# Vision tower: attention 1 value products in groups of four heads, 32 columns each, with the row sums in a bank of their own

## The chip, the cores and the metric

The kernel runs on one core of a Trainium2 chip. The time is the device time of one execution in microseconds (us). Before the change three runs took 4316.67, 4334.95 and 4337.84 us; the median is 4334.95 us.

## The reference

64 images pass through one block: patch embedding with two layer norms and a class token (197 tokens of 192 numbers), a first attention with 12 heads of 64 dims, and a second part that is a router with eight rank-16 adapters on the qkv projection and again an attention with 12 heads, of 16 dims each. Both halves are added to a residual. The change is in the first attention; its core is

```python
qkv = x @ w_qkv.T                       # (b, 197, 3 * 12 * 64)
q = q * rsqrt(norm over heads(q) + EPS) # k likewise
dots = einsum('bhid,bhjd->bhij', q, k)
scores = softmax(dots / scale[:, None, None], axis=-1)
out = einsum('bhij,bhjd->bhid', scores, v)
out = out.transpose(0, 2, 1, 3).reshape(b, n, h * dh) @ w_out.T + b_out
```

Here `h` is the head, `i` the query token, `j` the key token and `d` the dim.

## The kernel before

Everything is written by hand: one instruction stream per engine, with semaphores. The table `ORDER` lists the steps of half a pass; each engine walks through the same table and does its own part of every step. Half a pass is done for buffer set s = 0 and once more for s = 1, and a loop repeats the pair. A step with a minus sign belongs to the other set's image, so that two images are under way, half a pass apart: while the first attention of one runs, the second attention of the image before it, and the embedding of the one after it, run between its steps. `@n` is the PSUM bank of a step's product (there are eight); steps in `WIDE` take two banks.

The steps of the first attention that matter here, for pair i of heads 2i and 2i+1 (i = 0 to 5):

- `ST.i`: the scores with the keys as rows, 99 keys at a time (two key tiles t), on TensorE (lines 545 to 563); ScalarE then takes the exponential from PSUM into one of four buffers `ebuf` (line 732). The buffers go round over both attentions' exponentials.
- `PV.i` (line 574): TensorE multiplies the values with `ebuf`. The result has the dims in PSUM rows and the queries in columns: head e of the pair in rows 64e to 64e+63. One group of four matmuls (2 key tiles x 2 heads) gives the values; four more with a block of ones in place of the values (`ones_col`, 64 wide) give, in the same bank, the row sums, repeated in 64 rows. They are float32 and 197 columns wide. Each float32 matmul has two records of the profile, so a step of 8 matmuls shows as 16. Then ScalarE makes 1/sum as exp(-ln(sum)) (lines 740 and 741) into `rinv`.
- `M.i` (line 943): VectorE multiplies the two into `o_t`, which lies in the first half of `qk`.
- `OP` (line 586): the output projection, on six tiles of 128 rows of `o_t`.

The second attention's `PV2.i` (line 633) takes four heads at once, each in 32 columns (16 dims, 16 ones), and takes the sums out of the same product. `OP2` is its projection, `T1` the transposes of the next image, `LA`, `LB`, `LC` its layer norm steps on VectorE and GpSimd.

An engine does its steps strictly in the order of the table: a step of ScalarE that waits holds all the steps behind it.

Of the kernel before, what the change touches and what calls it, by code (L numbers as in the profile page):

```python
# [27 lines left out]
NT = NP + 1  # L28
PD, KC = 768, 6
TR, TO = 99, 98  # L30
# [18 lines left out]
-X -OP@2 QK.0@4 -LD -T2@3 QK.1@0 -G@7 QK.2@4 -GB S -EMB@7 -T3@2 PS@6 N.0 -QK2.0@6 N.1 -QK2.1@0  # L49
N.2 -V2@2 -SM2.0@4 -SM2.1@2 N.3 -SM2.2@0 V.0@4 -SM2.3@2 -SM2.4@0 -SM2.5@6 V.1@4 SM.0@0 -NT2@7  # L50
SM.1@2 SM.2@4 -ST2.0@0 SM.3@6 -ST2.1@2 SM.4@0 SM.5@4 -ST2.2@6 -PV2.0@3 -M2.0 NT@0 -ST2.3@6
-ST2.4@2 -ST2.5@4 -PV2.1@6 ST.0@0 -PV2.2@4 ST.1@2 -LA ST.2@6 PV.0@4 M.0 PV.1@5 ST.3@0 -M2.1
ST.4@2 PV.2@6 -LB M.1 -M2.2 ST.5@0 PV.3@2 M.2 M.3 PV.4@3 PV.5@6 M.4 -LC M.5 -OP2@1 -T1@3
"""


# [13 lines left out]
EMBEDDING = ("X", "EMB", "LA", "LB", "LC", "T1")  # L70
BEHIND = {p for p in SCHED[:len(SCHED) // 2] if p[1] == 1 and p[0] not in EMBEDDING}
AHEAD = {p for p in SCHED if p[1] == 0 and p[0] in EMBEDDING}
WIDE = ("QK", "V", "SM", "ST", "QK2", "SM2", "ST2")
EBUFS = 4


# [58 lines left out]
def vit_tower(nc, x_t, w_emb, ln1, ln1_bias, tok_const, tok_bias, w_qk, w_v, w_out, w_gl, w_qkv2, w_lora_b,  # L135
# [4 lines left out]
    with ctx:  # L140
        def sb(name, shape, dt=F32):
            return ctx.enter_context(nc.sbuf_tensor(name, shape, dt))
# [55 lines left out]
        ss = two("ss", [128, 2, NT])  # L198
        nrm = [ss[s][:].rearrange("p a t -> p (a t)") for s in range(2)]
        hn2_t = [ss[s][0:HC] for s in range(2)]  # L200
        vx_both = sb("vx", [TR, 2, 2, H, DH])
        vx = [vx_both[:, s] for s in range(2)]
        ones_col = sb("ones_col", [TR, DH])
        mx = two("mx", [TR, 2, H])
        neg = two("neg", [TR, 2, 128])
        ebuf = [sb(f"ebuf{i}", [TR, 2, 2, NT]) for i in range(EBUFS)]
# [78 lines left out]
        neg_copied = signal("neg_copied", ("NT2",))  # L285
        mx2_ready = signal("mx2_ready", ("NT2",))
        res_ready = rd_sig["OP2"]
        rr_ready = signal("rr_ready", ("PS",))
        rinv_ready = signal("rinv_ready", ("PV",))
        sums2_ready = rd_sig["PV2"]  # L290
# [29 lines left out]
        def passes(eng, body):  # L320
            body(Pass("start", -1))
            body(Pass("first", 0))
            with eng.Fori(1, ITERS - 1) as it:
# [2 lines left out]
            body(Pass("last", ITERS))  # L326

        loads = [(emb_raw, w_emb), (ln1_sb, ln1), (ln1b_raw, ln1_bias), (tokc, tok_const), (tok_b, tok_bias), (qk_raw, w_qk),
                 (v_raw, w_v), (out_w, w_out), (gl_w, w_gl), (qkv2_raw, w_qkv2), (lorab_raw, w_lora_b),
                 (bias2_raw, w_bias2), (proj_w, w_proj), (scale_sb, scale), (rowc, row_const),  # L330
                 (mats_sb, mats), (sel_raw[0:64], head_rows[64:128]), (sel_raw[64:128], head_rows[64:128])]
        e_order = [p for p in SCHED if p[0] in ("ST", "ST2")]
        pv_order, pv2_order = steps["made_PV"], steps["made_PV2"]

# [6 lines left out]
            return (xss_ready, p) if p[0] == "X" else (ss_ready, ("S", p[1], 0))  # L341

        def exp_used(p):
            q = ("PV", p[1], p[2]) if p[0] == "ST" else ("PV2", p[1], p[2] // 2)
            return pe_sig[q[0]], q

        def tile_cols(t):
# [101 lines left out]
        def _(pe):  # L449
# [34 lines left out]
            def body(now):  # L484
                for p in now.steps():
# [87 lines left out]
                                mm = nc.tensor.matmul(o, kb[s][:, h, tile_cols(t)], qb[s][:, g, 0:NT],  # L573
                                                      start=False, stop=True)
                    elif kind == "PV":
                        wait(pe, now, rd_sig["ST"], ("ST", s, i))
                        wait(pe, now, rd_sig["V"], ("V", s, 1))
                        eb = ebuf[e_order.index(("ST", s, i)) % EBUFS]
                        for at in (0, NT):
                            for t in range(2):  # L580
                                n = key_rows(t)
                                for e in range(2):
                                    left = vx[s][0:n, t, 2 * i + e, :] if at == 0 else ones_col[0:n]
                                    mm = nc.tensor.matmul(ps(p, slice(DH * e, DH * e + DH), slice(at, at + NT)),  # L584
                                                          left, eb[0:n, e, t, :], start=(t == 0), stop=(t == 1))
                    elif kind == "OP":
                        wait(pe, now, rd_sig["PV"], ("M", s, 5))
                        for t in range(2):
                            for m in range(H // 2):
                                mm = nc.tensor.matmul(ps(p, slice(0, TR), slice(D * t, D * t + D)),  # L590
# [65 lines left out]
        def _(act):  # L656
# [13 lines left out]
            def body(now):  # L670
                act.sem_clear(act_chain)
                count[0] = 0
                for p in now.steps():
# [36 lines left out]
                    elif kind == "N" and i % 2 == 1:  # L710

                        wait(act, now, qkn_ready, ("N", s, i - 1))
                        high = (qh, kh)[i // 2]
                        nc.scalar.copy(high[:, :, 0:NT], qk[s][:, 6 * (i // 2):6 * (i // 2) + 6, :]
                                       ).then_inc(high_N[1], 1)
                    elif kind == "V":
                        wait(act, now, pe_sig[kind], p)
                        nc.scalar.mul(  # L718
                            vx[s][:, i].rearrange("p (b h) d -> p b h d", b=2),
                            psum[0:TR, b:b + 2, 0:INNER // 2].rearrange("p b (h d) -> p b h d", d=DH),  # L720
                            1 / WS).then_inc(done, 1)
                    elif kind == "NT":
                        wait(act, now, pe_sig[kind], p)
                        nc.scalar.copy(neg_t[s][:, 0:NT], psum[:, b, 0:NT]).then_inc(done, 1)
                    elif kind == "NT2":
                        wait(act, now, pe_sig[kind], p)
                        nc.scalar.copy(qb[s][64:128, 0, 0:NT], psum[64:128, b, 0:NT]).then_inc(neg_copied[1], 1)
                    elif kind in ("ST", "ST2"):
                        wait(act, now, pe_sig[kind], p)
                        n = e_order.index(p)  # L730
                        wait_free(act, now, e_users[n % EBUFS], exp_used)
                        nc.scalar.activation(ebuf[n % EBUFS][:].rearrange("p e a t -> p e (a t)"),  # L732
                                             psum[0:TR, b:b + 2, 0:2 * NT], ACT.Exp).then_inc(done, 1)
                    elif kind == "PV":

                        wait(act, now, pe_sig[kind], p)
                        n = pv_order.index(p) % 2
                        wait_free(act, now, rinv_users[n], reader)
                        r = rinv[n][:]
                        link(nc.scalar.activation(r, psum[:, b, NT:2 * NT], ACT.Ln))  # L740
                        nc.scalar.activation(r, r, ACT.Exp, scale=-1.0).then_inc(rinv_ready[1], 1)  # L741
                    elif kind == "PV2":
                        wait(act, now, sums2_ready, p)
                        r = sums2[pv2_order.index(p) % 2][:]
                        link(nc.scalar.activation(r, r, ACT.Ln))
                        nc.scalar.activation(r, r, ACT.Exp, scale=-1.0).then_inc(rinv2_ready[1], 1)
                    elif kind == "G":

                        wait(act, now, gmax_ready, p)
                        nc.scalar.activation(gates[s][:, :, 0:NE], gl[s][:, :, 0:NE], ACT.Exp  # L750
                                             ).then_inc(gexp_ready[1], 1)
                    elif kind == "T3":
                        wait(act, now, pe_sig[kind], p)
                        nc.scalar.copy(comb_t[s][:, 0:NT], psum[0:3 * (NE + 1), b, NT:2 * NT])
                        nc.scalar.copy(hw_s[s][:, 0, 0:NT], psum[:, b, 0:NT]).then_inc(split_T3[1], 1)
                    elif kind == "QK2":
                        wait(act, now, pe_sig[kind], p)

                        dst, f = (qa[s], QSCALE / WS) if i == 0 else (high2, 1 / WS)
                        if i == 1:  # L760
                            wait_free(act, now, high2_users, reader)
                        nc.scalar.mul(dst[:, 0:2, 0:NT],
                                      psum[:, b, 0:2 * NT].rearrange("p (m t) -> p m t", m=2), f)
                        nc.scalar.mul(dst[:, 2, 0:NT], psum[:, b + 1, 0:NT], f).then_inc(high_QK2[1], 1)
                        if i == 1:

                            wait(act, now, high_QK2, p)
                            for j in range(4):
                                a = nc.scalar.mul(ka[s][:].rearrange("p (g j) t -> p g j t", j=4)[:, :, j, :],  # L769
                                                  high2[:], masks[:, j:j + 1])  # L770
# [10 lines left out]
        def _(dve):  # L781
# [59 lines left out]
            def body(now):  # L841
                dve.sem_clear(dve_chain)
                count[0] = 0
                for p in now.steps():
# [92 lines left out]
                    elif kind == "M":  # L937
                        done, q = rd_sig["PV"][1], ("PV", s, i)
                        b = BANK[q]

                        wait(dve, now, rinv_ready, q)
                        r = rinv[pv_order.index(q) % 2]
                        nc.vector.tensor_tensor(o_t[s][:, i, :], psum[:, b, 0:NT], r[:], ALU.mult  # L943
                                                ).then_inc(done, 1)
                    elif kind == "OP":

# [162 lines left out]
```

## Time and profile before

| | before |
|---|---|
| median of three runs | 4334.95 us |
| the profiled execution's own time | 4333.73 us |
| its span (first to last instruction) | 4331.8 us |
| TensorE matmuls busy | 3840.3 us, 89% |
| VectorE busy | 2706.7 us, 62% |
| ScalarE busy | 2232.1 us, 52% |
| GpSimd busy | 524.0 us, 12% |
| mean granted TensorE clock | 0.953 |

The profile is of one execution. Busy time is the union of an engine's instructions. Matmuls overlap each other in the record, and the time of one record is not its cost: the distance from the start of a group of them to the start of the next is.

### The profile page before, as it was taken

The page shows a single profiled execution, that of the slowest core. Times are in us where ns is not written, and L with a number is a line of the kernel's source. Part 1 is how long each engine was busy: PE and PEld are TensorE (multiplying, and loading weights), DVE is VectorE, ACT ScalarE, POOL GpSimd, SP SyncE. Part 2 cuts the span into 40 slices and gives each one's busy share as a digit, 9 for nine tenths or more (in the row PEclk, how much of TensorE's full clock was granted, in tenths as well). Part 3 has the DMA queues.
Part 4 walks back from the last instruction along what each step waited for, and adds up shares of the span by engine and source line. Part 5 has one row for each costly group of instructions (what it writes and reads, how often), then busy time and mean ns, then how long its engine had stood idle before and what let it go on. Part 6 is the DMA issues. An engine that isn't in the chain of part 4 may idle for free.

```text
span 4331.8 us, 98533 instructions
## 1 busy us (share of the span) xinstructions
PE 3840.3 (89%) x38552; PEld 3175.7 (73%) x38552; DVE 2706.7 (62%) x6866; ACT 2232.1 (52%) x3969; POOL 524.0 (12%) x858
## 2 busy tenths in 40 slices
PE   4999998889988998989999889899888898899888
PEld 3777777777777777777777777777777777777776
DVE  4666666566566666665665666666656656656654
ACT  1555555555555555545545555555555555555553
POOL 1110111111101101101111011011111111111110
PEclk7999999999999999999999999999999999999997
DMA  2000000000000000000000000000000000000000
GB/s 76 8 16 8 16 8 15 15 10 14 15 8 15 16 8 15 15 8 15 8 15 16 8 15 15 8 16 15 9 15 10 14 15 10 14 15 8 15 4 4
DMA packets 26198, 60.41 MB, mean 14 GB/s; under 512 B 3534, under 2 KB 16465, under 8 KB 25714
## 3 DMA queue, kind: packets, MB, share of 16 engines
q1 hardware_dynamic: 25806, 54.14, 4.1%
q8 instruction: 377, 6.18, 0.6%
q14 instruction: 15, 0.09, 0.0%
HBM read 44.45 MB, written 9.68 MB: 12 GB/s over the span
## 4 chain that ended last, share of the span: by engine, by line
PE 72%; DVE 17%; issue 4%; ACT 4%; POOL 1%; DMA 0%; SPq 0%; DVEq 0%; ACTq 0%; POOLq 0%
PE psum L584 13%; DVE mx L922 9%; PE psum L590 7%; PE psum L513 6%; PE psum L523 6%; PE psum L618 6%; PE psum L496 6%; PE psum L557 5%; PE psum L541 3%; PE psum L648 3%; PE psum L641 2%; PE psum L620 2%; PE psum L621 2%; ACT ka L769 2%; PE psum L571 2%
## 5 line engine op out<-in xcount | busy, mean ns | idle before, releaser
L922 DVE TENSOR_REDUCE mx<-psum 99x4 f32<-99x788 f32 x768 | 707.2, 972 | 67.3 <-PE psum L541 40.3
L732 ACT ACTIVATE ebuf<-psum 99x788 f32<-99x788 f32 x768 | 605.8, 825 | 175.7 <-PE psum L573 163.9
L513 PE MATMUL psum<-hn_s,qk_w 96*128 96x197 f16 x4608 | 435.8, 252 | 1.2 <-DVE hn_s L888 1.2
L440 POOL TENSOR_TENSOR veps<-mv,eps_ln 99x2 f32<-99x2 f32 x256 | 49.9, 195 | 3169.2 <-DVE mv L831 2552.9
L696 ACT ACTIVATE qk_sq<-psum 128x788 f32<-128x788 f32 x192 | 159.1, 828 | 516.0 <-PE psum L513 516.0
L513 PEld LDWEIGHTS psum<-hn_s,qk_w 96*128 96x128 f16 x4608 | 406.2, 99 | 8.8 <-DVE hn_s L888 1.5
L618 PE MATMUL psum<-hn_s,qkv_w 96*128 96x197 f16 x2304 | 342.2, 254 | 44.2 <-ACT ss L705 43.1
L523 PE MATMUL psum<-v_w,hn_s 96*99 96x384 f16 x1536 | 333.6, 376 | 30.3 <-DVE mx L922 21.8
L943 DVE TENSOR_TENSOR qk<-psum,rinv 128x197 f32<-128x197 f32 x384 | 137.9, 359 | 342.1 <-ACT rinv L741 342.1
L590 PE MATMUL psum<-out_w,qk 128*99 128x192 f32 x1536 | 286.8, 348 | 61.5 <-issue 61.3
L584 PE MATMUL psum<-ebuf,vx 98*64 98x197 f32 (+1 forms) x3072 | 332.6, 336 | 0.0
L571 PE MATMUL psum<-qa,ka 128*99 128x197 f16 x1536 | 288.9, 252 | 46.8 <-DVE qb L934 31.3
L584 PE MATMUL psum<-ebuf,ones_col 98*64 98x197 f32 (+1 forms) x3072 | 323.3, 330 | 0.0
L590 PEld LDWEIGHTS psum<-out_w,qk 128*99 128x99 f32 x1536 | 264.9, 178 | 72.1 <-issue 66.4
L541 PE MATMUL psum<-ka,qa 128*99 128x197 f16 x1536 | 209.7, 298 | 110.5 <-ACT ka L769 100.7
L523 PEld LDWEIGHTS psum<-v_w,hn_s 96*99 96x99 f16 x1536 | 216.3, 147 | 113.8 <-DVE mx L922 29.9
L620 PE MATMUL psum<-hw_s,lorab_w 128*128 128x197 f16 x1152 | 290.7, 252 | 0.0
L718 ACT ACTIVATE vx<-psum 99x768 f32<-99x768 f32 x128 | 103.9, 812 | 352.6 <-PE psum L523 352.6
L573 PE MATMUL psum<-qb,kb 128*99 128x197 f16 x1536 | 282.7, 248 | 0.0
L541 PEld LDWEIGHTS psum<-ka,qa 128*99 128x99 f16 x1536 | 182.0, 156 | 133.7 <-issue 55.4
L496 PE MATMUL psum<-emb_w,xb 128*99 128x193 f32 x1536 | 263.9, 327 | 12.6 <-DVE emb_b L821 12.6
L618 PEld LDWEIGHTS psum<-hn_s,qkv_w 96*128 96x128 f16 x2304 | 189.2, 99 | 116.8 <-ACT ss L705 83.3
(164 smaller groups left out, 8006.3 us busy)
## 6 DMA issues: line engine op xcount, KB each, us to landing
xb<-x_t SPq DMA_DIRECT2D x64, 591.0 KB, 3.8
out<-h SPq DMA_DIRECT2D x128, 73.5 KB
vx<-w_qk SPq DMA_DIRECT2D x1, 1152.0 KB
out<-h SPq DMA_DIRECT2D x64, 0.8 KB
qk<-w_qkv SPq DMA_DIRECT2D x1, 720.0 KB
qk_sq<-w_emb SPq DMA_DIRECT2D x1, 576.0 KB
v_raw<-w_v SPq DMA_DIRECT2D x1, 576.0 KB
out_w<-w_out SPq DMA_DIRECT2D x1, 576.0 KB
```

Of the source, the lines that this page charges most:

```text
L496: nc.tensor.matmul(ps(p, slice(0, TR), slice(194 * t, 194 * t + D + 1)), xb[s][:, c, tile_cols(t)], emb_w[:, c, :], start=(c == 0), stop=( ...
L513: mm = nc.tensor.matmul(ps(p, slice(0, 128), slice(at, at + NT), m // 2), qk_w[:, w, c, f:f + 128], hn_s[s][:, v, c, 0:NT], start=(n == 0) ...
L523: mm = nc.tensor.matmul(ps(p, slice(0, TR), slice(0, INNER // 2), b), hn_s[s][:, v, c, tile_cols(i)], v_w[:, w, c, INNER // 2 * b:INNER // ...
L541: mm = nc.tensor.matmul(ps(p, slice(0, TR), slice(NT * t, NT * t + NT), e), qa[s][:, h // 4, tile_cols(t)], ka[s][:, h, 0:NT], start=True, ...
L571: nc.tensor.matmul(o, ka[s][:, h, tile_cols(t)], qa[s][:, g, 0:NT], start=True, stop=False)
L573: mm = nc.tensor.matmul(o, kb[s][:, h, tile_cols(t)], qb[s][:, g, 0:NT], start=False, stop=True)
L584: mm = nc.tensor.matmul(ps(p, slice(DH * e, DH * e + DH), slice(at, at + NT)), left, eb[0:n, e, t, :], start=(t == 0), stop=(t == 1))
L590: mm = nc.tensor.matmul(ps(p, slice(0, TR), slice(D * t, D * t + D)), o_t[s][:, m, tile_cols(t)], out_w[:, m, :], start=(m == 0), stop=(m ...
L618: nc.tensor.matmul(o, qkv2_w[:, w, c, f], hn2_s[s][:, v, c, 0:NT], start=(c + w + v == 0), stop=False)
L620: nc.tensor.matmul(o, lorab_w[:, w, f], hw_s[s][:, v, 0:NT], start=False, stop=False)
L732: nc.scalar.activation(ebuf[n % EBUFS][:].rearrange("p e a t -> p e (a t)"), psum[0:TR, b:b + 2, 0:2 * NT], ACT.Exp).then_inc(done, 1)
L922: nc.vector.tensor_reduce(mx[s][:, :, 2 * i:2 * i + 2].rearrange("p a e -> p e a"), psum[0:TR, b:b + 2, 0:2 * NT].rearrange("p e (a t) -> ...
```

## The change

The six `PV` steps of an image become three, each over four heads. A head's 64 dims are taken in two halves of 32 (c = 0, 1). Head j of the four has the 32 PSUM rows 32j to 32j+31, for both halves and for the sums; the halves stand side by side in the first bank, the sums (c = 2) alone in the second. The sums are made first and have a semaphore of their own (`sums_made`), on which ScalarE waits. VectorE's multiply takes both halves at once, with one `rinv` for both, and waits for the values too. The dims of `o_t` stand in another order now, so the rows of `out_w` are loaded in that order, by eight DMAs in place of one, at the end of the list of loads. A step now needs the exponentials of two `ST` steps. In the table the three new steps stand behind `ST.2`, `ST.4` and `ST.5`.

```diff
--ST2.4@2 -ST2.5@4 -PV2.1@6 ST.0@0 -PV2.2@4 ST.1@2 -LA ST.2@6 PV.0@4 M.0 PV.1@5 ST.3@0 -M2.1
-ST.4@2 PV.2@6 -LB M.1 -M2.2 ST.5@0 PV.3@2 M.2 M.3 PV.4@3 PV.5@6 M.4 -LC M.5 -OP2@1 -T1@3
+-ST2.4@2 -ST2.5@4 -PV2.1@6 ST.0@0 -PV2.2@4 ST.1@2 -LA ST.2@6 PV.0@4 M.0 ST.3@0 -M2.1
+ST.4@2 PV.1@6 -LB M.1 -M2.2 ST.5@4 PV.2@2 -LC M.2 -OP2@1 -T1@7
-WIDE = ("QK", "V", "SM", "ST", "QK2", "SM2", "ST2")
+WIDE = ("QK", "V", "SM", "ST", "PV", "QK2", "SM2", "ST2")
-        ones_col = sb("ones_col", [TR, DH])
+        ones_col = sb("ones_col", [TR, DH // 2])
+        sums_made = signal("sums_made", ("PV",))
         loads = [...
-                 (v_raw, w_v), (out_w, w_out), (gl_w, w_gl), ...
+                 (v_raw, w_v), (gl_w, w_gl), ...
+        for j in range(4):
+            for c in range(2):
+                loads.append((out_w[32 * j:32 * j + 32, c::2, :],
+                              w_out[64 * (j % 2) + 32 * c:64 * (j % 2) + 32 * c + 32, j // 2::2, :]))
                     elif kind == "PV":
-                        wait(pe, now, rd_sig["ST"], ("ST", s, i))
+                        wait(pe, now, rd_sig["ST"], ("ST", s, 2 * i + 1))
                         wait(pe, now, rd_sig["V"], ("V", s, 1))
-                        eb = ebuf[e_order.index(("ST", s, i)) % EBUFS]
-                        for at in (0, NT):
+                        for c in (2, 0, 1):
                             for t in range(2):
                                 n = key_rows(t)
-                                for e in range(2):
-                                    left = vx[s][0:n, t, 2 * i + e, :] if at == 0 else ones_col[0:n]
-                                    mm = nc.tensor.matmul(ps(p, slice(DH * e, DH * e + DH), slice(at, at + NT)),
-                                                          left, eb[0:n, e, t, :], start=(t == 0), stop=(t == 1))
+                                for j in range(4):
+                                    eb = ebuf[e_order.index(("ST", s, 2 * i + j // 2)) % EBUFS]
+                                    left = (vx[s][0:n, t, 4 * i + j, 32 * c:32 * c + 32] if c < 2
+                                            else ones_col[0:n])
+                                    mm = nc.tensor.matmul(
+                                        ps(p, slice(32 * j, 32 * j + 32), slice(NT * (c % 2), NT * (c % 2) + NT), c // 2),
+                                        left, eb[0:n, j % 2, t, :], start=(t == 0), stop=(t == 1))
+                            if c == 2:
+                                mm.then_inc(sums_made[1], 1)
...
-                        wait(act, now, pe_sig[kind], p)
+                        wait(act, now, sums_made, p)
...
-                            link(nc.scalar.activation(r, psum[:, b, NT:2 * NT], ACT.Ln))
+                            link(nc.scalar.activation(r, psum[:, b + 1, 0:NT], ACT.Ln))
...
                         wait(dve, now, rinv_ready, q)
+                        wait(dve, now, pe_sig["PV"], q)
-                        nc.vector.tensor_tensor(o_t[s][:, i, :], psum[:, b, 0:NT], r[:], ALU.mult
+                        nc.vector.tensor_tensor(o_t[s][:, 2 * i:2 * i + 2, :],
+                                                psum[:, b, 0:2 * NT].rearrange("p (c t) -> p c t", c=2),
+                                                r[:].unsqueeze(1).broadcast_to([128, 2, NT]), ALU.mult
```

Two places show what moves. The first is TensorE's stream in the loop's half pass for s = 1, around the end of `ST.2` and `PV.0`. `ebuf2`, `ebuf3`, `ebuf0`, `ebuf1` hold the exponentials of `ST.0`, `ST.1`, `ST.2`, `ST.3` there; `vx` are the values. Before:

```order
L561 MATMUL psum<-neg_t1,head_sel 99x197 x2
L584 MATMUL psum<-ebuf2,vx 64x197 x4
L584 MATMUL psum<-ebuf2,ones_col 64x197 x4
L584 MATMUL psum<-ebuf3,vx 64x197 x4
L584 MATMUL psum<-ebuf3,ones_col 64x197 x4
L557 MATMUL psum<-qh,kh 99x197 x2
```

and of the change (line 584 is line 591 now, 557 is 563, 561 is 567):

```order
L567 MATMUL psum<-neg_t1,head_sel 99x197 x2
L591 MATMUL psum<-ebuf2,ones_col 32x197 x2
L591 MATMUL psum<-ebuf3,ones_col 32x197 x2
L591 MATMUL psum<-ebuf2,ones_col 32x197 x2
L591 MATMUL psum<-ebuf3,ones_col 32x197 x2
L591 MATMUL psum<-ebuf2,vx 32x197 x2
L591 MATMUL psum<-ebuf3,vx 32x197 x2
L591 MATMUL psum<-ebuf2,vx 32x197 x2
```

The step started with `ebuf2` alone and came to `ebuf3` after eight matmuls; now `ebuf3` is needed by the third matmul, and the step waits for it ahead of its first.

The second place is ScalarE's stream from the exponential of `ST.1` on (`ebuf3`), in the loop's half pass for s = 0. Before:

```order
L732 ACTIVATE ebuf3<-psum 99x788
L308 REGISTER_ALU
L732 ACTIVATE ebuf0<-psum 99x788
L740 ACTIVATE rinv0<-psum 128x197
L741 ACTIVATE rinv0<-rinv0 128x197
L740 ACTIVATE rinv1<-psum 128x197
L741 ACTIVATE rinv1<-rinv1 128x197
L308 REGISTER_ALU
L732 ACTIVATE ebuf1<-psum 99x788
L308 REGISTER_ALU
L732 ACTIVATE ebuf2<-psum 99x788
```

and of the change (732 is 742, 740 and 741 are 750 and 751, the register instruction of 308 is that of 310):

```order
L742 ACTIVATE ebuf3<-psum 99x788
L310 REGISTER_ALU
L742 ACTIVATE ebuf0<-psum 99x788
L750 ACTIVATE rinv0<-psum 128x197
L751 ACTIVATE rinv0<-rinv0 128x197
L310 REGISTER_ALU
L742 ACTIVATE ebuf1<-psum 99x788
L310 REGISTER_ALU
L742 ACTIVATE ebuf2<-psum 99x788
L750 ACTIVATE rinv1<-psum 128x197
L751 ACTIVATE rinv1<-rinv1 128x197
```

The order of the exponentials is as it was; the second pair of `rinv` instructions ahead of `ebuf1` is gone. Over a half pass three pairs are left of six.

## Rows read from the trace of the kernel before

**Rows 1.** The page: busy time, and the chain that ended last by engine and line.

```profile
PE 3840.3 (89%) x38552; PEld 3175.7 (73%) x38552; DVE 2706.7 (62%) x6866; ACT 2232.1 (52%) x3969; POOL 524.0 (12%) x858
...
PE 72%; DVE 17%; issue 4%; ACT 4%; POOL 1%; DMA 0%; SPq 0%; DVEq 0%; ACTq 0%; POOLq 0%
```

**Rows 2.** Chain of waits, one half pass's value products (start us, us, what).

```profile
2081.58 0.86 PE psum L641 x16
2082.44 0.39 PE psum L557 x6
...
2083.25 0.81 PE psum L641 x16
...
2085.55 2.84 PE psum L584 x32
...
2089.89 1.49 PE psum L584 x16
...
2092.19 4.18 PE psum L584 x48
2096.37 2.12 PE psum L648 x12
```

**Rows 3.** TensorE's timeline, same half pass (start us, us, what, idle before).

```profile
2085.49 0.89 PE L584 MATMUL psum<-ebuf,vx 98*64 98x197 f32 x8
2086.21 0.84 PE L584 MATMUL psum<-ebuf,ones_col 98*64 98x197 f32 x8
```

**Rows 4.** ScalarE's timeline, same half pass.

```profile
2085.63 0.81 ACT L732 ACTIVATE ebuf<-psum 99x788 f32<-99x788 f32 x1
...
2089.25 1.55 ACT L732 ACTIVATE ebuf<-psum 99x788 f32<-99x788 f32 x2
2091.42 0.34 ACT L740 ACTIVATE rinv<-psum 128x197 f32<-128x197 f32 x1 [0.63 <-PE psum L584]
...
2092.24 0.83 ACT L732 ACTIVATE ebuf<-psum 99x788 f32<-99x788 f32 x1
```

**Rows 5.** ScalarE's timeline, an exponential for which TensorE waits.

```profile
2080.63 0.83 ACT L732 ACTIVATE ebuf<-psum 99x788 f32<-99x788 f32 x1
```

**Rows 6.** TensorE's weight loads that waited for it.

```profile
2081.53 0.35 PEld L641 LDWEIGHTS psum<-ebuf,v 98*32 98x32 f32 x12 [0.16 <-ACT ebuf L732]
```

**Rows 7.** VectorE's timeline, the half pass of rows 2.

```profile
2088.42 0.66 DVE L837 TENSOR_SCALAR h<-hn,mv,rstd 99x192 f32<-99x192 f32 x2
...
2090.95 0.25 DVE L831 BATCH_NORM_AGGREGATE mv<-st 99x2 f32<-99x6 f32 x2
```

**Rows 8.** Groups (line, engine, op, shapes, count | busy us, mean ns | idle before).

```profile
L943 DVE TENSOR_TENSOR qk<-psum,rinv 128x197 f32<-128x197 f32 x384 | 137.9, 359 | 342.1 <-ACT rinv L741 342.1
...
L888 DVE TENSOR_TENSOR hn_s<-psum,hn_s 96x394 f16<-96x394 f32 x128 | 72.5, 567 | 120.3 <-ACT hn_s L690 120.3
...
L641 PEld LDWEIGHTS psum<-ebuf,v 99*32 99x32 f32 x1536 | 53.0, 111 | 11.5
```

**Rows 9.** Timeline of the program's start: DMA issues, VectorE's first work.

```profile
3.87 0.42 SPq L360 DMA_DIRECT2D out_w<-w_out  x1
...
8.62 3.85 SPq L360 DMA_DIRECT2D qk_sq<-sel  x2
...
27.25 1.36 DVE L792 TENSOR_TENSOR emb_w<-qk_sq,ln_sb 128x1152 f32<-128x1152 f32 x1 [27.25 <-DMA qk_sq<-sel]
```

**Rows 10.** Half passes (us; busy PE, PEld, DVE, ACT, POOL; PEclk; DMA).

```profile
3294.74:3360.50 65.76, 57.62 (x605) 47.57 (x603) 41.87 (x108) 34.90 (x62) 8.41 (x14) 1.00 0.06 19
3360.50:3424.18 63.68, 58.67 (x605) 48.74 (x603) 41.98 (x107) 34.80 (x62) 7.77 (x13) 0.97 0.03 7
1837.33:1906.87 69.54, 62.07 (x605) 50.95 (x603) 41.98 (x107) 34.90 (x62) 8.43 (x14) 0.93 0.06 19
```

**Rows 11.** TensorE's timeline, behind three of its longest waits.

```profile
1862.79 1.52 PE L541 MATMUL psum<-ka,qa 128*99 128x197 f16 x12 [1.59 <-ACT ka L769]
1864.71 4.08 PE L523 MATMUL psum<-v_w,hn_s 96*99 96x384 f16 x12 [0.41 <-DVE mx L922]
...
2042.54 0.52 PE L480 MATMUL psum<-mats_sb,hn 98*96 98x98 f32 x4 [1.46 <-DVE hn L837]
...
2070.48 2.15 PE L523 MATMUL psum<-v_w,hn_s 96*99 96x384 f16 x12
```

**Rows 12.** Granted clock of stretches of TensorE (us; busy; PEclk; DMA).

```profile
1862.00:1863.00 1.00, 0.21 (x3) 1.00 0.00 0
...
1864.00:1869.00 5.00, 4.59 (x17) 0.50 0.00 0
...
2085.49:2096.30 10.81, 10.81 (x146) 1.00 0.01 3
```

**Rows 13.** The line that ends OP on VectorE, once per half pass.

```profile
L950 DVE TENSOR_TENSOR h<-psum,h x64: 557/558/559, 122.2 to 4277.2; 99x384 f32<-99x384 f32 x64
```

More of the change, by code:

```diff
@@ L328, in vit_tower @@
         loads = [(emb_raw, w_emb), (ln1_sb, ln1), (ln1b_raw, ln1_bias), (tokc, tok_const), (tok_b, tok_bias), (qk_raw, w_qk),
-                 (v_raw, w_v), (out_w, w_out), (gl_w, w_gl), (qkv2_raw, w_qkv2), (lorab_raw, w_lora_b),
+                 (v_raw, w_v), (gl_w, w_gl), (qkv2_raw, w_qkv2), (lorab_raw, w_lora_b),
                  (bias2_raw, w_bias2), (proj_w, w_proj), (scale_sb, scale), (rowc, row_const),
                  (mats_sb, mats), (sel_raw[0:64], head_rows[64:128]), (sel_raw[64:128], head_rows[64:128])]
+        for j in range(4):
+            for c in range(2):
+                loads.append((out_w[32 * j:32 * j + 32, c::2, :],
+                              w_out[64 * (j % 2) + 32 * c:64 * (j % 2) + 32 * c + 32, j // 2::2, :]))
         e_order = [p for p in SCHED if p[0] in ("ST", "ST2")]
@@ L343, in exp_used @@
         def exp_used(p):
-            q = ("PV", p[1], p[2]) if p[0] == "ST" else ("PV2", p[1], p[2] // 2)
+            q = ("PV", p[1], p[2] // 2) if p[0] == "ST" else ("PV2", p[1], p[2] // 2)
             return pe_sig[q[0]], q
@@ L575, in body @@
                     elif kind == "PV":
-                        wait(pe, now, rd_sig["ST"], ("ST", s, i))
+                        wait(pe, now, rd_sig["ST"], ("ST", s, 2 * i + 1))
                         wait(pe, now, rd_sig["V"], ("V", s, 1))
-                        eb = ebuf[e_order.index(("ST", s, i)) % EBUFS]
-                        for at in (0, NT):
+                        for c in (2, 0, 1):
                             for t in range(2):
                                 n = key_rows(t)
-                                for e in range(2):
-                                    left = vx[s][0:n, t, 2 * i + e, :] if at == 0 else ones_col[0:n]
-                                    mm = nc.tensor.matmul(ps(p, slice(DH * e, DH * e + DH), slice(at, at + NT)),
-                                                          left, eb[0:n, e, t, :], start=(t == 0), stop=(t == 1))
+                                for j in range(4):
[7 more added lines that the diff above has]
+                                mm.then_inc(sums_made[1], 1)
                     elif kind == "OP":
-                        wait(pe, now, rd_sig["PV"], ("M", s, 5))
+                        wait(pe, now, rd_sig["PV"], ("M", s, 2))
                         for t in range(2):
```

## The prediction, made before the changed kernel ran

> **What bounds the kernel now.** I read the page first: matmuls are busy 89% of the span, and the chain that ended last runs 72% over TensorE, 17% over VectorE and 4% over ScalarE [rows 1]. So a microsecond matters if it lies on TensorE's stream, and in stretches where TensorE does not itself wait. Then I read the chain of waits in the stretch of the value products. It stays on TensorE from end to end: step after step, without a wait, from PV2 to the end of the six PV steps and on to OP2 (L648) [rows 2]. There TensorE alone sets the pace, and ScalarE follows it: it is idle 0.63 us before a 1/sum [rows 4]. Shorter value products would therefore shorten every half pass in full, unless a new wait appears. There are 64 half passes, one per image.
>
> **The value products on TensorE.** The six steps stand in three groups of the chain, of two, one and three steps: 2.84, 1.49 and 4.18 us, together 8.51 us [rows 2]. Each further step adds 1.345 us, ((4.18 - 1.49) / 2), so a group has 0.145 us at its start and 8 matmuls of 64 columns take 1.345 us. The price of 32 columns is in PV2, which already puts four heads side by side: 8 matmuls, 0.81 us [rows 2], less the 0.145 us at the start 0.665 us, half of the wide ones. A new step has 24 such matmuls: 0.145 + 3 x 0.665 = 2.14 us; three steps 6.42 us. Gain 8.51 - 6.42 = 2.09 us per image, 134 us in all. This is what the change would bring if nothing else moved. The unknown is whether the rate of PV2 holds over 24 matmuls in a row; below it can't go (197 columns are streamed at the same pace), above it could come to one weight load after the other, 111 ns each [rows 8], two records per matmul: 48 x 0.111 = 5.33 us per step. I take the rate of PV2, because its 16 loads, at the same 111 ns each, are within its 0.81 us, and 12 of them take 0.35 us together [rows 6].
>
> The row shows that the loads of neighbouring column groups overlap. The Trainium skill says otherwise (TensorE: Matmul & The Clock Gate, Part 3, The mechanism): weight loads overlap running matmuls only if they are for other rows of the array, and all of these take the same rows. By that rule the step would come to the 5.33 us above. The trace disagrees with it in PV2; I keep it as a rival for the longer run.
>
> **The waits that it adds.** TensorE stops for a step until the exponentials of two ST steps are there, not one. What comes behind it in its stream (the next ST, and with it the next exponential) stops too. I move the stretch of [rows 2] through, with these durations: from the end of an exponential to the effective start of the step that waits for it 0.17 us (exponential over at 2080.63 + 0.83 = 2081.46 [rows 5], the step behind it over at 2082.44, and it takes 0.81 [rows 2]: 2082.44 - 0.81 - 2081.46); an exponential 0.83 us, the last one of ST.5 starting 0.86 us after ST.5 itself (2092.24 [rows 4], 2089.89 + 1.49 = 2091.38 [rows 2]); ST.5 0.81 us (2092.19 - 2091.38), ST.3 and ST.4 together 1.50 us (2089.89 - 2088.39).
> - PV.0 could start at 2085.55. It needs the exponential of ST.1, which ScalarE runs from 2085.63 to 2086.44 [rows 4]; it starts at 2086.61. Wait 1.06 us. Before, TensorE was at the first pair's products meanwhile [rows 3]. It ends at 2088.75.
> - ST.3 and ST.4 run to 2090.25. The exponential of ST.3 starts 0.86 us after ST.3, at 2089.61, and ends at 2090.44. PV.1 starts at 2090.61: wait 0.36 us; it ends at 2092.75.
> - ST.5 runs to 2093.56. Its exponential runs from 2093.61 to 2094.44, and PV.2, the very next step, needs it: start 2094.61, wait 1.05 us, end 2096.75. Before, three steps were left here and only the last needed ST.5.
>
> OP2 starts at 2096.75 and not at 2096.37 [rows 2]. The three waits (2.47 us) eat the gain (2.09 us) and 0.38 us more. Times 64 this is +24 us. The waits scale with nothing that the change makes faster: each is one exponential and its hand-over, behind an ST that TensorE has just made.
>
> **The other parts.** ScalarE has three pairs of 1/sum fewer, and starts them when the sums are made. It takes work from an engine that waits for TensorE here; the exponentials that TensorE now waits for don't stand behind the removed pairs (ST.1's is ahead of them, ST.3's starts when its scores are made). Gain nothing; had ScalarE been late it would be 0.34 to 0.7 us. VectorE's six multiplies of 0.359 us become three over 394 columns, at the 0.567 us of such a read from PSUM [rows 8]: 0.45 us less per image, off the path. But M.0 now waits for the values to 2088.8 and holds LB behind it: LB begins about 2089.8 (0.57 and M2.1 later) and not at 2088.42, and takes 2.8 us to its last instruction (2088.42 to 2091.20 [rows 7]), so to 2092.6; M.1 can't begin before that anyway. LC follows at about 2094, and T1, which needs it, comes behind OP2 at 2098.9. The last M.2 ends by 2097.5, OP starts behind OP2 and T1 (2096.75 + 2.12 + about 0.35), some 1.7 us later. These cost nothing; that 1.7 us is the cover. Banks: a step takes two, all of them free in time (ST.5 takes bank 4 when M.0 has long read it). The rows of `ones_col` and the order of `out_w` change no count.
>
> The start: all engines wait for the last constant, at 27.25 us. Seven more DMAs are issued behind what is last now. An issue takes 0.42 us for `out_w`, and 3.85 us for the two of `sel` [rows 9]: +2.9 us, between 0 (bandwidth is the limit) and 13 (7 x 1.9). I take 2.9, the row of the same tensor.
>
> **The sum.** It is made against the profiled execution's 4333.73 us (span 4331.8 and 1.9 around it), which is 1.2 us under the median of the three runs: 4333.7 + 24.3 + 2.9 = 4361 us. A change under 0.5%, 22 us, can't be told from none here; 4361 is 26 us over the median, so just beyond.
>
> **The clock.** The granted clock decides between kinds of half passes. Of equal work, two in a row took 65.76 and 63.68 us at clock 1.00 and 0.97, another of the first kind 69.54 us at 0.93 [rows 10]. The low clock (1.2 GHz for 2.4) sets in soon after TensorE's longest waits: after 1.59 us idle the clock was 0.50 for 5 us, and the twelve matmuls of L523 took 4.08 us for 2.15; after a wait of 1.46 us elsewhere it stayed at full speed [rows 11, 12]. The same wait has it in one half pass and not in the next, so it hangs on how the waits fall in time, and a half pass of another length changes that. The mean half pass is (4277.2 - 122.2) / 63 = 65.95 us [rows 13], a pair 131.9, between the quick pair (65.76 + 63.68 = 129.4) and the slow one (69.54 + 63.68 = 133.2). In the value products themselves the clock was 1.00 with TensorE never idle [rows 12]; the new waits, at most 1.06 us with 2.1 us of work or more between them, are shorter than those in front of a low clock.
>
> The Trainium skill (TensorE: Matmul & The Clock Gate, HAM oscillation) holds only waits longer than any in this loop for harmful. By it there would be no loss to shift; the trace disagrees, the clock falls after 1.59 us.
>
> **The rivals.**
> - The pairs become quick ones more often (faster side). All 32 quick: 32 x (131.9 - 129.4) = 80 us less than the forecast, 4281 us. For it: quick and slow pairs are about equally common now. Against: nothing in the change shortens the waits that bring the low clock. Half-way, 4321. It is faster beyond 0.5% from about two thirds of the way.
> - The pairs become slow ones more often: 32 x (133.2 - 131.9) = 42 us more, 4403 us. For it: three new waits.
> - The waits don't show, because the exponentials come earlier than I have them: 4333.7 - 134 + 2.9 = 4203 us. Against: [rows 4] has the start of ST.1's exponential fixed by ScalarE's order, untouched.
> - The narrow matmuls don't hold their rate over 24, up to loads one after another: 3 x 64 x (5.33 - 2.14) = 612 us more, 4973 us; from 2.26 us per step on it adds over 22 us. Against: PV2's rows.
> - The new waits bring the low clock once per image: 64 x (4.08 - 2.15) = 124 us more, 4485 us. Against: their length.
>
> **How the numbers follow.** The forecast, waits of 2.5 us against a gain of 2.1, has 0.60, with a range of its own of 4328 to 4390 (hand-over of 0.17 us left out three times is -33 us; an exponential 0.1 us later each time +19 and the start at 13 in place of 3 +10). Quick pairs 0.12, slow pairs 0.14, waits hidden 0.05, rate lost 0.04, low clock in the new waits 0.05. The range 4318 to 4405 leaves out the last three, and the far end of quick pairs. Slower than 4356.6 (+0.5%): 0.37 of my own case's 0.60, all but little of the 0.14, and 0.09, together 0.59. Faster than 4313: 0.05 and 0.09 of the quick pairs, 0.14. Same: 0.27.
>
> **What would show it.** Right: in TensorE's timeline a wait for the exponential (L742) of about 1 us before the first and the third value step, some 0.3 us before the second; a step of 48 records that takes 2.1 to 2.2 us; OP2 0.3 to 0.5 us later relative to the end of ST.2; about 150 us more of TensorE's idle time put down to ScalarE's exponential, and matmul busy time down by about 130 us. ScalarE busy down by 192 x 0.71 = 136 us with no effect. Wrong: waits under 0.5 us, value steps over 2.3 us, a granted clock off 0.953 by more than 0.01, or constants landing later than 32 us.

## The result: 2.1% slower, and the profile after

The changed kernel takes 4426.37 us (median of four runs, 4401.76 to 4442.45); the kernel before took 4336.4 us in the runs beside it (4316.67 to 4338.45). The ratio is 1.0213, 95% interval 1.0153 to 1.0273. Forecast were 4361 us, 4318 to 4405: the direction is right, and the loss is 90 us where 26 were expected. The profiled execution has a span of 4440.7 us against 4331.8.

The page of the changed kernel, busy time and the shares of the chain [rows 1]:

```profile
PE 3802.5 (86%) x41624; PEld 3145.2 (71%) x41624; DVE 2683.7 (60%) x6674; ACT 2096.0 (47%) x3585; POOL 523.8 (12%) x858
...
PE 67%; DVE 19%; ACT 7%; issue 5%; POOL 1%; SPq 0%; DMA 0%; DVEq 0%; ACTq 0%; POOLq 0%
```

ScalarE is down by the 136 us expected. TensorE's matmuls are down by only 38 us, though the value products alone went from 655.9 to 466.5 us: other matmuls took longer. One group of them, with not one matmul more, before and after:

```profile
L523 PE MATMUL psum<-v_w,hn_s 96*99 96x384 f16 x1536 | 333.6, 376 | 30.3 <-DVE mx L922 21.8 <-ACT vx L718 8.5
```

```profile
L529 PE MATMUL psum<-v_w,hn_s 96*99 96x384 f16 x1536 | 399.0, 430 | 48.7 <-DVE mx L932 40.1 <-ACT vx L728 8.5
```

The mean granted clock is 0.936, from 0.953.

The value products in the chain of waits, a stretch that answers to [rows 2] (start us, us, what):

```profile
3888.27 0.85 PE psum L651 x16
...
3890.65 0.81 ACT ebuf L742
3891.46 0.24 issue
3891.71 2.22 PE psum L591 x48
...
3894.78 0.84 ACT ebuf L742
3895.62 0.09 issue
3895.71 2.22 PE psum L591 x48
...
3898.79 0.84 ACT ebuf L742
3899.63 0.09 issue
3899.72 2.22 PE psum L591 x48
3901.94 2.12 PE psum L658 x12
```

In front of each value step the chain leaves TensorE for an exponential of ScalarE (L742). TensorE's timeline has the three waits, of 1.13, 0.29 and 0.97 us (in brackets, idle before the row):

```profile
3891.71 0.88 PE L591 MATMUL psum<-ebuf,ones_col 98*32 98x197 f32 x16 [1.13 <-ACT ebuf L742]
...
3895.71 0.88 PE L591 MATMUL psum<-ebuf,ones_col 98*32 98x197 f32 x16 [0.29 <-ACT ebuf L742]
...
3899.72 0.88 PE L591 MATMUL psum<-ebuf,ones_col 98*32 98x197 f32 x16 [0.97 <-ACT ebuf L742]
...
3901.87 2.19 PE L658 MATMUL psum<-proj_w,qk 128*99 128x192 f32 x12
```

Measured from ST.1's exponential, which begins at 3890.64 here and at 2085.63 in [rows 4], OP2 begins 11.23 us later where it began 10.67 us later (3901.87 - 3890.64; [rows 2] with the 0.07 us that the two views differ by): 0.56 us lost per half pass, where 0.38 were forecast. That is 36 us in 64 half passes at the most; the rest of the 90 must be elsewhere. Half passes, from the end of OP to the next, two pairs of one execution, the common kind first (columns as in [rows 10]):

```profile
1136.03:1202.48 66.45, 58.41 (x653) 48.39 (x651) 41.61 (x104) 32.67 (x56) 7.77 (x13) 0.95 0.03 7
1202.48:1272.49 70.01, 60.34 (x653) 49.93 (x651) 41.59 (x104) 32.78 (x56) 8.45 (x14) 0.93 0.05 17
3648.87:3714.32 65.45, 55.69 (x653) 46.24 (x651) 41.50 (x105) 32.77 (x56) 8.43 (x14) 1.00 0.06 20
3714.32:3778.58 64.26, 56.82 (x653) 47.38 (x651) 41.59 (x104) 32.68 (x56) 7.77 (x13) 0.97 0.03 7
1163.01:1169.84 6.83, 6.36 (x26) 4.92 (x27) 5.07 (x6) 1.55 (x2) 0.00 (x0) 0.50 0.00 0
1207.39:1210.80 3.41, 3.41 (x21) 3.25 (x19) 0.52 (x1) 1.44 (x2) 0.00 (x0) 0.50 0.02 5
1186.80:1198.60 11.80, 10.54 (x190) 8.97 (x183) 5.79 (x16) 4.49 (x10) 1.89 (x3) 1.00 0.01 3
```

The quick pair takes 65.45 + 64.26 = 129.71 us, 0.27 us more than the quick pair of before (129.44, [rows 10]). But most pairs, some 20 of 31, are of another kind, 66.45 + 70.01 = 136.46 us, which the trace of the kernel before does not have: its slow pairs mostly took 133.2, its longest 135.1. The last three rows say where: the clock is at half speed (0.50, 1.2 GHz) for 6.8 us from 27 us behind OP on, and for 3.4 us from 5 us behind it, while in the stretch with the value products and their new waits it is 1.00. TensorE's timeline at the first place shows what stands ahead of it:

```profile
1161.54 1.21 PE L547 MATMUL psum<-ka,qa 128*99 128x197 f16 x12 [1.66 <-ACT ka L779]
1163.48 4.08 PE L529 MATMUL psum<-v_w,hn_s 96*99 96x384 f16 x12 [0.73 <-DVE mx L932]
```

It is the wait of SM2.0 for `ka`; the one in [rows 11] is of 1.59 us, with the same 4.08 us behind it. The change does not touch these steps. Nor does the wait bring the low clock each time: in the quick pair of the same execution it stands there too, and the twelve matmuls of L529 take 2.15 us.

```profile
3674.31 1.20 PE L547 MATMUL psum<-ka,qa 128*99 128x197 f16 x12 [1.58 <-ACT ka L779]
3676.24 2.15 PE L529 MATMUL psum<-v_w,hn_s 96*99 96x384 f16 x12 [0.73 <-DVE mx L932]
```

The line that ends OP gives the mean, (4385.8 - 121.2) / 63 = 67.69 us per half pass, 1.74 more than the 65.95 of before [rows 13]; 1.74 x 63 = 110 us are the whole difference of the two spans (109 us).

```profile
L963 DVE TENSOR_TENSOR h<-psum,h x64: 556/558/559, 121.2 to 4385.8; 99x384 f32<-99x384 f32 x64
```

The start of the program has little to do with it: the last constant lands 1.2 us later than in [rows 9].

```profile
28.42 1.36 DVE L802 TENSOR_TENSOR emb_w<-qk_sq,ln_sb 128x1152 f32<-128x1152 f32 x1 [28.42 <-DMA out_w<-w_out]
```

### The profile page after: what moved, and what is told of

It reads as the page before. It is cut to its first block, busy times and chain, and to the rows that moved or that the text cites. A ratio compares the mean times of both kernels' runs of the same rounds, so it can differ in the third digit from the quotient of the medians.

```text
span 4440.7 us, 104158 instructions
## 1 busy us (share of the span) xinstructions
PE 3802.5 (86%) x41624; PEld 3145.2 (71%) x41624; DVE 2683.7 (60%) x6674; ACT 2096.0 (47%) x3585; POOL 523.8 (12%) x858
## 4 chain that ended last, share of the span: by engine, by line
PE 67%; DVE 19%; ACT 7%; issue 5%; POOL 1%; SPq 0%; DMA 0%; DVEq 0%; ACTq 0%; POOLq 0%
PE psum L591 10%; DVE mx L932 9%; PE psum L529 8%; PE psum L519 7%; PE psum L600 6%; PE psum L628 6%; PE psum L502 6%; ACT ebuf L742 4%; PE psum L658 3%; PE psum L547 3%; PE psum L563 3%; PE psum L651 2%; PE psum L630 2%; DVE kb L1030 2%; PE psum L610 2%
## 5 line engine op out<-in xcount | busy, mean ns | idle before, releaser
L742 ACT ACTIVATE ebuf<-psum 99x788 f32<-99x788 f32 x768 | 605.3, 825 | 344.1 <-PE psum L567 182.2
L519 PE MATMUL psum<-hn_s,qk_w 96*128 96x197 f16 x4608 | 454.1, 257 | 1.2 <-DVE hn_s L898 1.2
L529 PE MATMUL psum<-v_w,hn_s 96*99 96x384 f16 x1536 | 399.0, 430 | 48.7 <-DVE mx L932 40.1
L519 PEld LDWEIGHTS psum<-hn_s,qk_w 96*128 96x128 f16 x4608 | 419.3, 101 | 12.5 <-DVE hn_s L898 1.5
L529 PEld LDWEIGHTS psum<-v_w,hn_s 96*99 96x99 f16 x1536 | 250.3, 170 | 160.0 <-DVE mx L932 53.2
L954 DVE TENSOR_TENSOR qk<-psum,rinv 128x394 f32<-128x394 f32 x192 | 109.2, 569 | 367.0 <-PE psum L591 367.0
L600 PE MATMUL psum<-out_w,qk 128*99 128x192 f32 x1536 | 261.6, 327 | 44.5 <-issue 44.2
L591 PE MATMUL psum<-ebuf,vx 98*32 98x197 f32 (+1 forms) x6144 | 298.3, 330 | 0.0
L591 PE MATMUL psum<-ebuf,ones_col 98*32 98x197 f32 (+1 forms) x3072 | 168.2, 334 | 151.8 <-ACT ebuf L742 151.5
L600 PEld LDWEIGHTS psum<-out_w,qk 128*99 128x99 f32 x1536 | 245.0, 166 | 49.8 <-issue 49.2
L547 PEld LDWEIGHTS psum<-ka,qa 128*99 128x99 f16 x1536 | 191.0, 161 | 125.8 <-issue 55.1
```

The costliest lines, as they stand in the source:

```text
L519: mm = nc.tensor.matmul(ps(p, slice(0, 128), slice(at, at + NT), m // 2), qk_w[:, w, c, f:f + 128], hn_s[s][:, v, c, 0:NT], start=(n == 0) ...
L529: mm = nc.tensor.matmul(ps(p, slice(0, TR), slice(0, INNER // 2), b), hn_s[s][:, v, c, tile_cols(i)], v_w[:, w, c, INNER // 2 * b:INNER // ...
L547: mm = nc.tensor.matmul(ps(p, slice(0, TR), slice(NT * t, NT * t + NT), e), qa[s][:, h // 4, tile_cols(t)], ka[s][:, h, 0:NT], start=True, ...
L591: mm = nc.tensor.matmul(ps(p, slice(32 * j, 32 * j + 32), slice(NT * (c % 2), NT * (c % 2) + NT), c // 2), left, eb[0:n, j % 2, t, :], sta ...
```

## The experiments

Two questions were put: how much of the 90 us is the clock, and what moves it. Two tools serve them. A filler is a row of matmuls whose result the step itself overwrites:

```python
def fill(p, n):
    for _ in range(n):
        nc.tensor.matmul(ps(p, slice(0, 128), slice(0, NT)), qk_w[:, 0, 0, 0:128],
                         qk_w[:, 0, 0, 0:NT], start=True, stop=True)
```

Put ahead of a wait, and no longer than it, it fills idle time and adds nothing to the chain; put behind it (a padding) it is added work.

**1. The kernel before, padded by four matmuls.**

```diff
                         wait(pe, now, o2_ready, ("M2", s, 2))
+                        fill(p, 4)
```

> The kernel before, with four more float16 matmuls of 197 columns (they write OP2's own bank, which OP2 then overwrites) in front of the six projections of OP2, once per half pass: about 0.34 us of matmuls and up to 0.15 us for one more change between float16 and float32, so 0.34 to 0.5 us later from OP2 on. That is about the delay that the change has at the same place (0.56 us in its trace). Theory A (the loss is mostly the clock: any small delay per half pass moves the loop into an alignment in which the low clock comes in both half passes): clearly more than the 22 to 32 us of the added work, 40 to 100 us over the kernel before, with a granted clock under 0.950. Theory B (the new waits for the exponentials themselves, or the narrow matmuls, cost the 90 us): 22 to 32 us, clock 0.953 as before.

Measured: 4327.94 us against 4326.64 for the kernel before on the same chip, ratio 1.0005 (0.9984 to 1.0026), clock 0.955. Neither came: not the 22 us of work, and not the loss. That any small delay upsets the clock is false; theory A was narrowed to: some delays do, and which ones can't be told beforehand.

**2 and 3. Both kernels with fillers.**

```diff
+                        if i == 0:
+                            fill(p, 18)
                         wait(pe, now, rd_sig["QK2"], ("QK2", s, 1))
...
+                        fill(p, 16)
                         wait(pe, now, hn2_ready, ("LD", s, 0))
```

> The kernel before, with matmuls whose result is overwritten put in front of two waits of TensorE: 18 (about 1.53 us) ahead of the wait of SM2.0 (1.66 us idle in the trace), 16 (1.36 us) ahead of the wait of T2 (1.46 us idle). They add no time to the chain if the wait is as long as they are. Theory A: the granted clock rises well over 0.953, and the time falls by the clock losses, to the length of quick half passes: 60 to 90 us less than before, 4245 to 4280 us. Theory B says nothing of this kernel beyond: no change, or a few us more.

> The changed kernel with the same fillers as the kernel before got (18 matmuls ahead of SM2.0's wait, 16 ahead of T2's). Theory A: with the clock out of the way, what is left is the change's own cost: 15 to 40 us over the kernel before with fillers, so some 4270 to 4310 us, 110 to 150 us under the changed kernel. Theory B: about 90 us over the kernel before with fillers.

Measured: 4268.37 us (4267.58 to 4271.61; ratio to before 0.987, 0.9854 to 0.9887) and 4273.86 us (4272.27 to 4275.41; 0.9885, 0.9868 to 0.9901). So the fillers take 58 us off the one and 152 us off the other, although they add matmuls. Half passes of each, the kernel before with fillers first; its first two rows are its common pair, the third is the second half pass of one of the nine pairs in 31 that still hold some low clock:

```profile
2134.75:2198.30 63.55, 60.41 (x639) 50.47 (x638) 41.87 (x108) 34.73 (x62) 7.77 (x13) 1.00 0.02 6
2198.30:2264.09 65.79, 60.51 (x639) 50.45 (x637) 41.88 (x107) 34.84 (x62) 8.41 (x14) 1.00 0.06 20
2067.60:2134.76 67.16, 62.20 (x639) 51.81 (x637) 41.89 (x108) 34.84 (x62) 8.41 (x14) 0.97 0.06 19
```

```profile
2001.89:2065.97 64.08, 58.55 (x687) 49.15 (x686) 41.52 (x104) 32.65 (x56) 7.74 (x13) 1.00 0.03 8
2065.97:2131.56 65.59, 58.66 (x687) 49.14 (x685) 41.51 (x104) 32.74 (x56) 8.40 (x14) 1.00 0.06 19
```

The first half pass of the pair, at full clock in both, is 0.53 us longer with the change: the 0.56 us of above. In the second it is not. There the loop starts over, and TensorE stands at the first step behind the branch (OP) with nothing of the profile to wait for ("issue"; that its instructions are not there yet is my reading, no view shows it). The views of waits, the kernel before and the change, then both with fillers:

```profile
PE psum L590 <- issue: 61.3, 29, 2.5
```

```profile
PE psum L600 <- issue: 44.2, 29, 1.8
```

```profile
PE psum L597 <- issue: 59.6, 29, 2.4
```

```profile
PE psum L607 <- issue: 40.4, 29, 1.8
```

A TensorE that comes later waits 17 to 19 us less there. So 29 of the 64 half passes, those behind the branch, hide their 0.56 us, and the other 35 lose it: about 20 us, an estimate. The two kernels with fillers are only 5.5 us apart because the one before still loses some time to the clock: its nine pairs are about 1.6 us longer than its others, 15 us in all, and 5.5 + 15 comes to the same 20 us. Of the 90 us that the change costs, about 20 are thus its own waits and about 70 the clock.

**4. The change with an order that covers the exponentials.**

```diff
--ST2.4@2 ... ST.1@2 -LA ST.2@6 PV.0@4 M.0 ST.3@0 -M2.1
-ST.4@2 PV.1@6 -LB M.1 -M2.2 ST.5@4 PV.2@2 -LC M.2 -OP2@1 -T1@7
+-ST2.4@2 ... ST.1@2 -LA ST.2@6 ST.3@0 PV.0@4 M.0 -M2.1
+-LB ST.4@2 ST.5@6 PV.1@0 M.1 -M2.2 -LC PV.2@4 M.2 -OP2@1 -T1@7
```

> The changed kernel with the order moved so that other work of TensorE covers the exponentials: PV.0 behind ST.3 (not ST.2), PV.1 and PV.2 behind ST.5, in banks 0 and 4, ST.5 in bank 6, LB behind M.0. By the timeline PV.1 and PV.2 no longer wait, PV.0 some 0.3 us. Waits of 2.4 us per half pass in the change's trace become 0.3. Both theories: TensorE's idle time before L591 put down to the exponential falls from 151 us to 20 us or so. Theory A: 2.1 us x 64 = 134 us less work on the chain than in the change, plus or minus some 60 us of clock: 4230 to 4350 us. Theory C (the narrow matmuls do not hold their rate and the waits only stand where TensorE would have stood anyway): within 20 us of the changed kernel.

Measured: 4241.22 us (4222.32 to 4249.7), ratio to before 0.9815 (0.9794 to 0.9835). The waits fell as said, in the view of waits of this kernel and of the change:

```profile
PE psum L591 <- ACT ebuf L742: 28.2, 63, 0.6
```

```profile
PE psum L591 <- ACT ebuf L742: 151.5, 191, 1.3
```

Theory C falls: the waits were real, and taking them away makes the narrow products pay. The kernel is 185 us quicker than the change, more than the 134 us of waits; its granted clock is higher as well, 0.951 for 0.936, so this run does not price the order alone. Experiment 8 does.

**5, 6 and 12. The changed kernel padded by 4, 8 and 12 matmuls; 9 and 10, the kernel before by 8 and 12; 11, the kernel before with fillers and 8.**

> The changed kernel with the four overwritten matmuls in front of OP2 that the kernel before got in the first experiment, where they cost 1 us against 22 to 32 us of work. Theory A, as the first experiments left it (the loop falls into one alignment of its waits or another, and which one it is decides over the low clock): the padded kernel does more work and can come out anywhere between 4290 us (hardly any low clock) and 4450 us; a time clearly under the changed kernel's 4426 us would be shown by nothing else. Theory B (the time follows the work): 4426 + 22 to 32 = 4448 to 4458 us.

> The same with eight such matmuls, 0.68 to 0.83 us per half pass. Theory A: again a time that does not follow the work, 4310 to 4470 us, and different from the kernel with four by something other than 22 us. Theory B: 4426 + 44 to 53 = 4470 to 4479 us.

> The kernel before with eight overwritten matmuls in front of OP2 (0.68 to 0.83 us of work per half pass, 44 to 53 us in all). With four it came out 1 us slower where the work was 22 to 32 us. Theory A (alignment decides): again not the work's 44 to 53 us; with luck 0, with bad luck over 100 us. If the kernel before has no bad alignment at all (theory D: the changed kernel loses more to the clock whatever its alignment): 4324 + 30 to 60 us.

> The same with twelve: 1.02 to 1.17 us of work per half pass, 65 to 75 us. Theory A: one of the paddings of the kernel before should meet an alignment as bad as the changed kernel's, 100 us or more of clock loss beyond the 57 us that it has: over 4440 us here or with eight. Theory D: 4324 + 50 to 85 us.

> The kernel before with both fillers, and with eight overwritten matmuls in front of OP2. With hardly any low clock left, time should follow work: 4268 us plus 44 to 53 us, 4312 to 4321 us. This prices the padding itself. If it costs less than 30 us, the padding is hidden by something, and the padded kernels say less than I take from them.

> The changed kernel with twelve overwritten matmuls in front of OP2, 65 to 75 us of work. With none it took 4426 us, with four 4479 us, with eight 4434 us. Its own cost without clock losses would be 4274 + 65 to 75 = 4344 us. Theory A: some padding should bring the loss down to the 57 us of the kernel before, that is to about 4400 us. Theory D: its losses stay at 110 us or more: 4454 us or more.

| matmuls added per half pass | 0 | 4 | 8 | 12 |
|---|---|---|---|---|
| before | 4323 to 4336 | 4327.94 | 4470.60 | 4447.77 |
| ratio to before | 1 | 1.0005 (0.9984 to 1.0026) | 1.0332 (1.03 to 1.0365) | 1.0298 (1.0257 to 1.0339) |
| change | 4426.37 | 4479.14 | 4434.36 | 4448.71 |
| ratio to before | 1.0213 (1.0153 to 1.0273) | 1.036 (1.0343 to 1.0377) | 1.0256 (1.0239 to 1.0273) | 1.0286 (1.0247 to 1.0324) |
| before, with fillers | 4268.37 | | 4280.08 | |

With fillers eight matmuls cost 12 us; I had expected 44 to 53, and had written that under 30 us something hides the padding. It does: the first half pass of a pair takes the whole 0.6 to 0.7 us, the second hides it in the branch wait (59.6 to 43.4 us), and the nine pairs with some low clock are gone. So the work behind the paddings is small, and the time of the kernels without fillers does not follow it: with eight matmuls the kernel before loses 143 us, with four of them nothing; the changed kernel with eight is 45 us quicker than with four. The changed kernel with four, 4479 us, lies above both ranges written down for it (4290 to 4450 and 4448 to 4458): the clock can cost it more than I had allowed. Theory D falls: the kernel before, untouched but for eight matmuls, meets a pair like that of the change (its half passes, windows as above):

```profile
2097.34:2164.12 66.78, 61.12 (x613) 50.48 (x612) 41.99 (x108) 34.73 (x62) 7.79 (x13) 0.95 0.03 7
2164.12:2233.80 69.68, 62.87 (x613) 51.89 (x611) 41.98 (x108) 34.83 (x62) 8.43 (x14) 0.93 0.05 18
```

66.78 + 69.68 = 136.46 us, at clocks 0.95 and 0.93, the sum and the clocks of the changed kernel's common pair. In the traces of both kernels most pairs are near 129.5, 133.2 or 136.5 us, and the next pair is often of the same kind. It is no rule for the padded ones: the changed kernel goes to and fro between 132.4 and 137.2 us with eight matmuls, and has pairs of 131.6 to 138.0 us with twelve. The expectation for the changed kernel with twelve, that some padding brings its loss down to that of the kernel before, was not met by any of the three, and 4449 us is under the 4454 that theory D asked for too.

**7. Which of the two waits.** The change with the filler ahead of SM2.0's wait alone.

```diff
+                        if i == 0:
+                            fill(p, 18)
                         wait(pe, now, rd_sig["QK2"], ("QK2", s, 1))
```

> The changed kernel with only the 18 overwritten matmuls ahead of SM2.0's wait (1.6 us idle), and none ahead of T2's. In the changed kernel's trace the low clock begins at two places of a half pass: 27 to 29 us behind the end of OP, right behind SM2.0's wait (in both halves of a pair), and 5 us behind it, after T2's wait (in one of them). Theory A: the first is the costly one (6.8 us of low clock twice per pair, against 3.4 once), so this filler alone brings most of the 152 us between the changed kernel and the one with both fillers: 4280 to 4340 us. If the lock of both is needed: 4380 us or more.

Measured: 4280.82 us (4277.97 to 4283.55), ratio to before 0.9897 (0.988 to 0.9915), clock 0.985. 146 of the 152 us are gone by filling this one wait of about 1.6 us.

**8. Both together.**

> The changed kernel with the order that hides the exponentials and with both fillers. If the two act on their own, the waits' part is what the reordering took away from TensorE's idle time (151 to 28 us before L591, 123 us) and comes off the 4274 us of the changed kernel with fillers: about 4150 us, to be compared with 4268 us of the kernel before with fillers. That would make the narrow matmuls worth their 2.1 us per half pass: 4268 - 64 x 1.8 = 4153 us. If the narrow matmuls were not worth that, 4200 us or more.

Measured: 4121.38 us (4117.11 to 4123.96), ratio to before 0.9529 (0.9512 to 0.9546): the quickest kernel of the study, 4.7% under the kernel before and some 7% under the change. Its value steps in TensorE's timeline:

```profile
1978.88 0.88 PE L598 MATMUL psum<-ebuf,ones_col 98*32 98x197 f32 x16 [0.45 <-ACT ebuf L750]
...
1982.53 0.88 PE L598 MATMUL psum<-ebuf,ones_col 98*32 98x197 f32 x16
1983.22 1.53 PE L598 MATMUL psum<-ebuf,vx 98*32 98x197 f32 x32
1984.56 0.85 PE L598 MATMUL psum<-ebuf,ones_col 98*32 98x197 f32 x16
1985.23 1.53 PE L598 MATMUL psum<-ebuf,vx 98*32 98x197 f32 x32
1986.69 2.19 PE L666 MATMUL psum<-proj_w,qk 128*99 128x192 f32 x12
```

Two steps run back to back in 4.16 us (1982.53 to 1986.69). It is 152 us under the change with fillers, where 124 were expected from the waits alone; the 28 us more are not explained. Both kernels have almost no low clock in the loop, so the 152 us, 3.6%, are what the order is worth by itself.

## Where the prediction was right, and the step that failed

- **Bound, gain of the narrow products.** Right. A step was put at 2.14 us and took 2.15 (3899.72 to 3901.87 in TensorE's timeline; 2.22 in the chain, which counts from the release). The rate of four column groups holds over 48 records. The rule weighed there, that the weight loads could not overlap, is not borne out: 48 loads of 109 ns are 5.2 us end to end, and the step that holds them takes 2.15.

```profile
L591 PEld LDWEIGHTS psum<-ebuf,vx 98*32 98x32 f32 x3072 | 121.1, 109 | 7.9
```

- **The three waits.** Right: 1.06, 0.36 and 1.05 us forecast, 1.13, 0.29 and 0.97 us in the trace. Together with the steps 0.38 us per half pass were forecast and 0.56 are lost.
- **"Times 64 this is +24 us."** Close to the 20 us of above by luck: the loss per half pass was put too low, and 35 half passes bear it, not 64, since 29 begin behind the loop's branch, where TensorE waits anyway. That wait stood in the profile as "issue" before L590, 61.3 us in 29 waits; I had read it as a fixed cost.
- **Start.** 2.9 us forecast, 1.2 measured; the range held it.
- **The clock: the step that failed.** The sum kept the clock's losses as they were, a term of zero, and the rival for slow pairs was priced at 42 us with a chance of 0.14, with a pair of 133.2 us as the slowest. The changed kernel's common pair takes 136.46 us, with low clock in both half passes, and its mean pair, 135.4 us, is slower than the rival's worst. By the fillers the clock took 152 us of the changed kernel and, with the 15 us that they left, some 73 of the kernel before: of the 90 us 70 to 80 are this one term (90 - 20 by the runs, 152 - 73 by the fillers), and the rest, about 20, is near the 24 of the sum. The trace of the kernel before could have warned: it holds a slower pair than the one that I read, 135.1 us, with both half passes slow.

```profile
1174.57:1244.65 70.08, 62.05 (x605) 50.99 (x603) 41.98 (x107) 34.91 (x62) 8.44 (x14) 0.93 0.06 18
1244.65:1309.67 65.02, 59.96 (x605) 49.65 (x604) 41.97 (x108) 34.80 (x62) 7.78 (x13) 0.95 0.03 7
```

- **The signs.** One named for being wrong came in: the granted clock is off 0.953 by 0.017. Of those for being right, TensorE's idle time put down to the exponential came in (151.5 us for 150), and matmul busy time did not: it fell by 38 us and not by 130. What I did read right is that the new waits do not bring the low clock themselves: it is 1.00 in the stretch above, the records of L591 take 327 to 355 ns over the whole execution, and a filler at a wait which the change never touched takes 146 us back.
- The Trainium skill (TensorE: Matmul & The Clock Gate, HAM oscillation) has as its rule that only idle gaps longer than any in this loop do harm. These runs disagree: filling a wait of about 1.6 us is worth 146 us.

Not settled: which kind of pair a given kernel falls into. It is shown that the same wait has a low clock behind it in one half pass and not in another, and that eight matmuls elsewhere change how often. That it hangs on the time at which the wait comes fits this, and is not shown. I could not have said which number would do it, and got the first guess (four in the kernel before) wrong. Fillers show the size of the loss and do not explain the choice. Paddings other than 4, 8 and 12 matmuls, and at other places, were not tried.

## What to carry to other kernels

A step that does two steps' work needs both their inputs: count which of them is made last, and put other work of the waiting engine between; here that order, with the same matmuls, was worth 3.6% with the clock out of the way (4274 to 4121 us). Where TensorE waits over a microsecond in every turn of a loop and the clock row is not at 1.00, compare variants with those waits filled, because otherwise the clock can drown what they differ by: here 0.7 us of added work per half pass made one kernel 3.3% slower, and another one 1% quicker than half that work did. And fill them in the kernel that ships: 18 overwritten matmuls ahead of one wait took about 3% off.

## What was not expected of the hardware

- Adding work made a kernel quicker: 4479 us with four matmuls added per half pass, 4434 with eight.
- A turn of the loop costs TensorE about 2 us at the first step behind the branch (59.6 us in 29 waits), and a delay ahead of it is hidden there: eight added matmuls, 0.7 us each half pass, cost 12 us in 64 half passes and not 45.
